# Both transformer layers as one pipeline of tiles, eight slots a turn, with a table-driven Gelu

## The reference

```
h = layernorm(x);   x = x + self_attention(h) @ w_ao + b_ao        # 16 heads of 16, sequences of 64
h = layernorm(x);   x = x + cross_attention(h, ctx) @ w_co + b_co  # keys and values from ctx
h = layernorm(x);   x = x + gelu_tanh(h @ w1 + b1) @ w2 + b2       # hidden width 1024
attention: softmax(q k^T / 4 * mask - 10000 (1 - mask)) v
gelu_tanh(u) = 0.5 u (1 + tanh(0.79788 u (1 + 0.044715 u^2)))
```

## Time and profile before

| | us |
|---|---|
| median of the runs | 1342.52 |
| the profiled execution | 1332.95 |
| its span, first to last instruction | 1331.1 |
| TensorE busy | 1135.1 (85%) |
| VectorE busy | 916.7 (69%) |
| ScalarE busy | 568.9 (43%) |
| GpSimd busy | 437.8 (33%) |
| mean granted TensorE clock | 0.954 of 2.4 GHz |

### The profile page before, as it was taken

The page is one execution under the profiler, slowest core; times in us unless marked ns, Lnnn a source line. Parts: engine busy times, 40 slices in busy tenths (PEclk is TensorE's granted clock), DMA queues, the critical chain, the costliest instruction groups (busy, mean ns, idle before and its releaser), DMA issues. The chain is left out here.

```text
span 1331.1 us, 21107 instructions
## 1 busy us (share of the span) xinstructions
PE 1135.1 (85%) x7616; PEld 679.9 (51%) x7616; DVE 916.7 (69%) x1677; ACT 568.9 (43%) x1053; POOL 437.8 (33%) x387
## 2 busy tenths in 40 slices
PE   6985678988988988988988988958698998989976
PEld 5653446655656655655755655744332442523414
DVE  4883658749749749759659759564358777595674
ACT  3552435635645645645545545524122324313322
POOL 2110425225225225225225234130135435253240
PEclk9997799999999999999999999989789898998987
DMA  6130010010010020030010010030100010010100
GB/s 225 56 91 12 1 37 1 6 49 1 17 37 29 17 81 1 17 112 1 17 37 1 17 37 2 1 133 1 47 1 18 1 32 18 0 34 0 32 0 17
DMA packets 36651, 41.27 MB, mean 31 GB/s; under 512 B 8000, under 2 KB 32320, under 8 KB 36304
## 3 DMA queue, kind: packets, MB, share of 16 engines
q1 hardware_dynamic: 36432, 39.81, 9.4%
q0 software_dynamic: 128, 0.10, 0.0%
HBM read 31.52 MB, written 8.39 MB: 30 GB/s over the span
## 5 line engine op out<-in xcount | busy, mean ns | idle before, releaser
L614 POOL TENSOR_TENSOR b_rstd<-b_var,b_minus_half 128x1 f32<-128x1 f32 x64 | 43.2, 674 | 275.6 <-DVE b_var L1078 275.6
L609 POOL TENSOR_TENSOR b_sc<-b_sc,b_cross_add 128x1024 f32<-128x1024 f32 x32 | 75.5, 2359 | 159.2 <-DVE b_sc L1112 159.2
L828 PE MATMUL ps<-w,b_act_g 128*128 128x256 f32 x512 | 117.7, 381 | 2.9 <-DVE b_act_g L1152 2.8
L816 PE MATMUL ps<-b_hT,wl 128*128 128x512 f32 x256 | 117.9, 606 | 1.6 <-ACT b_hT L931 1.6
L1440 POOL TENSOR_TENSOR c_rs<-c_st,c_rF 128x512 f32<-128x512 f32 x64 | 82.2, 1287 | 107.5 <-DVE c_st L1858 107.5
L828 PEld LDWEIGHTS ps<-w,b_act_g 128*128 128x128 f32 x512 | 95.4, 190 | 22.0 <-DVE b_act_g L1152 6.6
L948 ACT ACTIVATE b_sc<-b_sc 128x1024 f32<-128x1024 f32 x64 | 68.0, 1062 | 84.2 <-DVE b_sc L1121 84.2
L678 PE MATMUL ps<-b_hT,wl 128*128 128x512 f32 x192 | 90.0, 613 | 5.9 <-ACT b_hT L931 5.9
L1119 DVE TENSOR_REDUCE b_neg_max<-b_sc 128x16 f32<-128x1024 f32 x64 | 77.6, 1212 | 20.3 <-POOL b_sc L609 20.0
L1121 DVE TENSOR_TENSOR b_sc<-b_sc,b_neg_max 128x1024 f32<-128x1024 f32 x64 | 88.5, 1382 | 2.2
L765 PE MATMUL ps<-ident,b_sc 128*128 128x128 f32 x512 | 70.4, 283 | 21.8 <-ACT b_sc L948 21.8
(11 more groups left out here) (175 smaller groups left out, 2333.5 us busy)
## 6 DMA issues: line engine op xcount, KB each, us to landing
b_x_in<-x_mid SPq DMA_DIRECT2D x8, 512.0 KB, 3.9
enc<-in_ctxT SPq DMA_DIRECT2D x8, 512.0 KB, 4.0
x_mid<-b_x_out SPq DMA_DIRECT2D x8, 512.0 KB, 2.9
wl<-in_wl SPq DMA_DIRECT2D x2, 1280.0 KB, 9.4
area<-in_wc SPq DMA_DIRECT2D x1, 2272.0 KB, 8.2
a_x_in<-in_x SPq DMA_DIRECT2D x16, 128.0 KB, 2.4
a_y_in<-in_ctx SPq DMA_DIRECT2D x16, 128.0 KB, 2.5
wl<-in_wl SPq DMA_DIRECT2D x2, 1024.0 KB, 8.6
```

What stands on the lines that cost most here:

```text
L609: pool.tensor_tensor(t, t, m, ALU.add).then_inc(add_ok, 1)
L816: mm = pe.matmul(ps[:, YB + j % 2, :], weight("w1", k, j * P, (j + 1) * P), hT[:, k, :], start=(k == 0), stop=(k == NC - 1))
L828: mm = pe.matmul(ps[:, YB + p % 2, 0:D], act_g[:, j, p * P:(p + 1) * P], w["w2"][:, j, :], start=(j == 0), stop=(j == NJ - 1))
```

## The change

Only `phase_b` and the division of the weights into sets change.

- Order: a turn is eight slots, k = 0 to 7: self tiles 0 to 3, then cross tiles 4 to 7 of the same group. Each slot does `probs_T(k)`, `out_project(k-1)`, `times_v(k)`, `scores(k+2)`, `result_T(k)` on TensorE. The loop has six passes; the first and the last turn stand outside.
- The layernorm between self and cross attention is done by tile: `norm_T_mid` and `queries_mid` of tile k-1 stand in slots 1 to 4, in bank CO, with 128 columns.
- Work that fills the slots: context keys and values in slots 0 and 1, the first MLP matrix of the previous group (`hidden`) in slots 1 to 4, the next group's input projections in slots 4 to 6, `mlp_out` in slots 5 to 7.
- Gelu: VectorE adds the bias from PSUM into `act_g`; ScalarE does `Gelu_apprx_tanh` in place over four chunks (2048 columns) at a time, in slots 3 and 4. The factor 0.5 in `result` goes.
- On VectorE `subtract_max` becomes `maximum` and `subtract`, with `residual` of the tile before between them.
- New buffers: `x_res` (x plus bias, so `x_in` is free early), own input norm buffers, `xc` twice, three `hT` in place of one. `pre` and `poly` go.
- Four weight sets in place of three: `last` is divided into `out` and `hidden`. SyncE's loop is written out.

The diff, cut to its core:

```diff
-SETS = {"first": 3, "middle": 3, "last": 4}
+SETS = {"first": 3, "middle": 3, "out": 2, "hidden": 3}
...
 # sync, around the change of layers
+            load_mask(4, mask_rows[0])
+            load_enc(4, enc_cols[0])
+            load_x(5, rows[1])
+            for done, count in ((k_ok[1], 2 * NG), (v_ok[1], 2 * NG), (q_ok[1], 2 * NP * NG), (bias_ok[1], NP * NG)):
+                sp.wait_ge(done, count)
+            reload("middle")
+            store(2, rows[2])
+            mark_ready("middle", 1)
+            sp.wait_ge(o_ps, tile(NG, 0))
+            sp.wait_ge(bias_ok[2], NP * NG)
+            reload("out")
...
+            sp.wait_ge(m_ps, NP * NG)
+            sp.wait_ge(pre_ok, NJ * NG)
+            reload("hidden")
+            store(3, rows[3])
+            mark_ready("hidden", 1)
...
 # gpsimd
+            def turn(n, prev, nxt):
+                for k in range(TILES):
+                    if k >= 1:
+                        inv_std(n, k - 1)
+                    elif prev is not None:
+                        inv_std(prev, TILES - 1)
+                    if nxt is not None and k == 1:
+                        inv_std_in(nxt)
+                    if k + 2 < TILES:
+                        add_mask(n, k + 2)
+                    elif nxt is not None:
+                        add_mask(nxt, k + 2 - TILES)
+                    ... # add_bias(n, k - 2), add_bias_in(nxt, k - 2)
...
 # tensor
+            def queries_mid(n, p):
+                pe.wait_ge(h_ok[1], tile(n, 2 * p) + 2)
+                for c in range(NC):
+                    for k in range(NC):
+                        mm = pe.matmul(ps[:, CO, D + c * P:D + (c + 1) * P], weight("q2", k, c * P, (c + 1) * P),
+                                       hT_mid[:, k, p * P:(p + 1) * P], start=(k == 0), stop=(k == NC - 1))
+                mm.then_inc(q_ps[1], 1)
+            def mlp_out(n, p, nxt):
+                if p == 0:
+                    pe.wait_ge(g_ok, 2 * n + 2)
+                if nxt is not None:
+                    pe.wait_ge((k_ok, v_ok)[p // 2][0], 2 * nxt + p % 2 + 1)
...
+            # turn(n, prev, nxt); begin(k): probs_T(k), out_project(k-1); middle(k): times_v(k), scores(k+2);
+            # end(k): norm_T_mid(k-1) for k = 1..4, result_T(k)
+            # 0: begin keys_ctx(n,0) middle keys_ctx(n,1) end values_ctx(n,0)
+            # 1: begin values_ctx(n,1) middle norm_T_mlp(prev) end hidden(0) queries_mid(0)
+            # 2: begin hidden(1) middle hidden(2) end hidden(3) queries_mid(1)
+            # 3: begin hidden(4) middle hidden(5) end hidden(6) queries_mid(2)
+            # 4: begin hidden(7) middle norm_T_in(nxt) end queries_in(nxt,0) queries_mid(3)
+            # 5: begin queries_in(nxt,1) middle keys_in(nxt,0) end keys_in(nxt,1) mlp_out(prev,0)
+            # 6: begin mlp_out(prev,1) middle values_in(nxt,0) end values_in(nxt,1)
+            # 7: begin mlp_out(prev,2) middle mlp_out(prev,3) end
...
 # scalar
-            def pre_square(n, j): ...
-            def tanh(n, j): ...
+            def gelu(n, half):
+                j = slice(half * NJ // 2, (half + 1) * NJ // 2)
+                act.wait_ge(pre_ok, NJ * n + j.stop)
+                t = act_g[:, j, :].rearrange("f j t -> f (j t)")
+                act.activation(t, t, ACT.Gelu_apprx_tanh).then_inc(g_ok, 1)
+            # slot 0: copy_pT exps(1) keys(1,n,0) copy_cT keys(1,n,1)
+            # slot 1: copy_pT exps(2) norm_out(2,prev) norm_out_mid(0) copy_cT
+            # slot 2: queries_mid(0) copy_pT exps(3) norm_out_mid(1) copy_cT
+            # slot 3: queries_mid(1) copy_pT exps(4) gelu(prev,0) norm_out_mid(2) copy_cT
+            # slot 4: queries_mid(2) copy_pT exps(5) gelu(prev,1) norm_out(0,nxt) norm_out_mid(3) copy_cT
+            # slot 5: queries_in(nxt,0) queries_mid(3) copy_pT queries_in(nxt,1) exps(6) keys(0,nxt,0) copy_cT
+            # slot 6: copy_pT keys(0,nxt,1) exps(7) copy_cT;   slot 7: copy_pT exps(nxt 0) copy_cT
...
 # vector
-                dve.scalar_tensor_tensor(t, t, 1.0 / GELU_B, pre[:, j % 4, :], ALU.add, ALU.mult).then_inc(arg_ok, 1)
-                dve.scalar_tensor_tensor(act_g[:, j, :], poly[:, j % 4, :], 1.0, pre[:, j % 4, :], ALU.add, ALU.mult).then_inc(g_ok, 1)
+                dve.tensor_scalar(act_g[:, j, :], ps[:, YB + j % 2, :], vec("b1", j), None, ALU.add).then_inc(pre_ok, 1)
+            # every slot k: maximum(k+1) residual(k-1) subtract(k+1) norm(k-1) normalize(k) mask(k+2), and with it
+            # 0: cross_masks at the end; 1: values(1,n,0) behind maximum, values(1,n,1) behind norm, stats_in(nxt) at the end
+            # 2: pre(0) behind maximum, pre(1) behind norm, pre(2) norm_in(nxt) at the end; 3: pre(3), pre(4), pre(5) likewise
+            # 4: pre(6), pre(7); 6: result(prev,0), result(prev,1), values(0,nxt,0) at the end
+            # 7: values(0,nxt,1) behind maximum, result(prev,2) behind norm, result(prev,3) at the end
```

More of the change, by code:

```diff
@@ L662, in _, with add_bias_in @@
-            inv_std_first(0)
-            self_attention(0, None)
-            with pool.Fori(0, TURNS - 1) as it:
-                inv_std_first(it + 1)
-                cross(it, it + 1)
-                self_attention(it + 1, it)
-            cross(TURNS - 1, None)
+            def add_bias_in(n, p):
+                pool.wait_ge(ld_x, 16 * n + 16)
+                if p == 0:
+                    pool.wait_ge(ready["first"], n + 1)
+                after(pool, res_ok, tile(n - 1, p + 1))
+                pool.tensor_tensor(x_res[:, p, :], x_in[:, p, :], row("bao"), ALU.add).then_inc(bias_ok[0], 1)
@@ L670, in _ @@
+            inv_std_in(0)
+            for p in range(NP):
+                add_bias_in(0, p)
+            add_mask(0, 0)
+            add_mask(0, 1)
+            turn(0, None, 1)
+            with pool.Fori(1, TURNS - 1) as it:
+                turn(it, it - 1, it + 1)
+            turn(TURNS - 1, TURNS - 2, None)
+            add_bias(TURNS - 1, TILES - 2)
+            inv_std(TURNS - 1, TILES - 1)
+            add_bias(TURNS - 1, TILES - 1)
         @block.tensor
@@ L906, in _, with begin, middle @@
-            first_norm_T(0)
+                mm.then_inc(m_ps, 1)
+            def begin(n, k, prev):
+                probs_T(n, k)
+                if k >= 1:
+                    out_project(n, k - 1)
+                elif prev is not None:
+                    out_project(prev, TILES - 1)
+            def middle(n, k, nxt):
+                times_v(n, k)
+                if k + 2 < TILES:
+                    scores(n, k + 2)
+                elif nxt is not None:
+                    scores(nxt, k + 2 - TILES)
@@ L907, in _ @@
+            norm_T_in(0, None)
             for c in range(2):
-                queries_1(0, c)
+                queries_in(0, c)
             for c in range(2):
-                keys_1(0, c)
+                keys_in(0, c)
+            scores(0, 0)
             for half in range(2):
-                values_1(0, half)
-            for c in range(2):
-                keys_2(0, c)
-            self_attention(0, None)
-            with pe.Fori(0, TURNS - 1) as it:
-                cross(it, it + 1)
-                self_attention(it + 1, it)
@@ L919, in _ @@
-            cross(TURNS - 1, None)
+                values_in(0, half, None)
+            scores(0, 1)
+            turn(0, None, 1)
+            with pe.Fori(1, TURNS - 1) as it:
+                turn(it, it - 1, it + 1)
+            n = TURNS - 1
+            turn(n, n - 1, None)
+            out_project(n, TILES - 1)
+            norm_T_mlp(n, None)
+            for j in range(NJ):
+                hidden(n, j)
+            for p in range(NP):
+                mlp_out(n, p, None)
         @block.scalar
@@ L1055, in _ @@
+            norm_out(0, 0)
+            for c in range(2):
+                queries_in(0, c)
+            for c in range(2):
+                keys(0, 0, c)
+            exps(0, 0)
+            turn(0, None, 1)
+            with act.Fori(1, TURNS - 1) as it:
+                turn(it, it - 1, it + 1)
+            n = TURNS - 1
+            turn(n, n - 1, None)
+            norm_out(2, n)
+            gelu(n, 0)
+            gelu(n, 1)
         @block.vector
@@ L1154, in result, with norm @@
+            def norm(n, k):
+                p = k % NP
+                dve.wait_ge(rstd_ok, tile(n, k) + 1)
+                dve.tensor_scalar(xc[:, k // NP, p, :], x_cur[:, p, :], mv[:, p, 0:1], rstd[:, p:p + 1], ALU.subtract, ALU.mult).then_inc(xc_ok, 1)
             def result(n, p):
@@ new lines, in last_residual, with last_norm, next_mask @@
+            def last_residual(n, k, prev):
+                if k >= 1:
+                    residual(n, k - 1)
+                elif prev is not None:
+                    residual(prev, TILES - 1)
+            def last_norm(n, k, prev):
+                if k >= 1:
+                    norm(n, k - 1)
+                elif prev is not None:
+                    norm(prev, TILES - 1)
```

(25 more changed lines are left out.)

971 lines of the change are left out of this document (464 added, 507 removed).

## The result

The changed kernel took 1358.39 us (median of four, 1357.82 to 1360.45), the kernel before 1342.62 beside it: +15.8 us, a ratio of 1.0115 with a 95% interval of 1.0095 to 1.0135. It is slower, by little but clear of the noise. The forecast was 1350, +7.5.

The account below looks back on a forecast made before the run. TensorE's work plus the holes between it was taken to bound the turn. Six turns +16, opening -3, last turn and tail -7, weights +2 gave +8: 1341 us profiled, 1350 as median, range 1304 to 1374.

Parts of the forecast that it names:

- TensorE's work and holes in a turn: Steady turn of the changed kernel: 85.9 us of TensorE work plus 13.1 of holes, 99.0 in all.
- clock in a turn: Steady turn: 3.2 us at half speed behind the hole before queries_in(0), +1.6 us.
- opening: First turn: context keys move into slot 0, then VectorE's cycle sets the slots; -3 us, bounds -12 and +8.
- last turn and tail: From the last turn to the transformer phase's end: 121 us against 128.2, -7, bounds -12 and +5.
- from the profiled execution to the median: Median of the kernel before lay 9.6 us above its profiled execution; the same was added for the changed kernel.
- slot 4's hole: TensorE waits for hT_in behind ScalarE's exps(5), load, gelu(1), norm_out(0): 3.4 us, 2.1 to 3.4 with the load's bounds.
- another +1.6: Slot 6, behind the 2.7 us hole before mlp_out(1): upper bound for a clock loss, for which nothing was taken.
- The loop edge's 1.9: Hole on TensorE at each loop edge, expected to stay 1.9 us as in the kernel before.
- the 0.8: Middle queries as 32 matmuls of 128 columns instead of 8 of 512: +0.8 us of TensorE work a turn.
- the two rivals on it: Table switch drains: slot 4's hole 4.7, 1358 us, 7%. Gelu shares Exp's table or loads hidden: 2.1, 1333 us, 20%.
- the drain's rival: A table load on busy ScalarE costs 1.3 us more: slot 4's hole 4.7, +8, 1358 us, 7%.
- ScalarE doesn't hold TensorE: hT_in and keys come in time, so slots 4 to 6 close: turn 91.9 us, 1298 in all, 20%.

Follow-up runs that it names:

- The experiment with transposes: Changed kernel with twelve transposes of the identity, results never read, in each of two holes, ahead of queries_in(0) and the second mlp_out: 1346.3 us.
- Tanh: Changed kernel with Tanh in place of Gelu in the two activations of 2048 columns, which computes another function: 1339.5 us.
- subtract first: Changed kernel with subtract ahead of residual in each slot on VectorE: 1338.9 us.
- the two orders: Changed kernel with keys(0,nxt,1) ahead of copy_pT(6) and the second Gelu behind copy_pT(5), both on ScalarE: 1321.6 us.
- the 1290 us kernel: Changed kernel with the four orders, subtract ahead of residual on VectorE, and values(1,n,1) ahead of norm(0) in slot 1: 1290.1 us.
- four orders: Changed kernel: keys(0,nxt,1) before copy_pT(6), second Gelu after copy_pT(5), add_mask(n,3) before inv_std_in(nxt), weights "middle" released before store(2): 1309.2 us.

## Why the prediction was wrong in size

The way the changed kernel loses time is the one forecast: holes at the places named, by the order on ScalarE, and the clock behind them. What was wrong in size is the clock term. Point by point, against the traced executions:

| step | forecast | traced |
|---|---|---|
| TensorE's work and holes in a turn | 99.0 | 99.0 (87.8 + 11.2) |
| clock in a turn | 1.6 | 3.4 |
| a turn | 100.6 (+2.7) | 102.4 (+4.8) |
| six turns, with the wait for weights | +18 | +28.8 |
| opening | -3 | +0.6 |
| last turn and tail | -7 | -4.5 |
| sum | +8 | +24.9 |
| from the profiled execution to the median: before, changed | 9.6, 9.6 | 9.6, 0.6 |

*The clock* is the step that failed: +1.6 a turn was given, for one loss, and 3.4 is what it cost, for two. The prediction let slot 4's hole lose it because it was as long as one that had, and gave slot 6 nothing, because a hole of 2.52 had kept it. Slot 4's hole proved to be 2.53, not 3.4, and both lost it, slot 6's in five of six turns. The bound of "another +1.6" was there and was not taken; it is 11 of the 17 us by which the traced sum was missed (opening and tail are the other 6). The experiment with transposes shows the size, 3.2. The price of one loss, 1.6, was right: 1.5 in slot 4, 1.7 in slot 6. That one hole kept the clock was no ground for zero, and the trace of before said so: the prediction has its steady turns at a clock of 1.00 throughout, which holds for the turn of the earlier trace rows, while another lost it behind 1.92 us (row at 478.67 above).

*The holes.* The sum of 99.0 was right in part by luck, by terms that offset each other: work 85.9 and holes 13.1 forecast, 87.8 and 11.2 traced. The same fault is in the account of before, whose 85.1 of work and 12.8 of holes are 87.1 and 10.6 in the mean of its six traced turns, so the difference between the kernels came out right. (The hidden chunks in it are 8 x 1.75 = 14.0, not 14.3, and the six loop edges of before are 1.4 to 1.9, not 1.9 each.) Slots 0, 1, 5 and 6 came near what was laid out (0.45, 1.11 + 1.16, 1.03, 2.55). Slot 4 was 0.9 shorter: exps(5) ended 5.7 us into the slot and hT_in was there at 10.3, as forecast, but TensorE wanted it at 7.8 and not at 7.0, 0.47 of that being its own wait for VectorE before `norm_T_in`. Slot 3, for which none above 0.2 had been given, had 0.84 and 0.71. The first is add_mask late by inv_std_in: it went with that order. The second went with Tanh and with subtract first; the first Gelu stands ahead of norm_out_mid(2) there, which the list of ScalarE's order already showed. The loop edge's 1.9 did not come. The middle queries in 128 columns took 0.9 a tile and so cost nothing more, but all of TensorE's busy time at full clock is 87.8 where the earlier trace rows have 86.85; the 0.8 was about right, by luck, and where the 0.9 lies is open.

*The opening* was 3.6 worse: one hole of 5.67 in slot 2, in which 3.3 had been allowed; GpSimd's order accounts for 2.9. *The tail* gave 4.5 of the 7, and moves by more than that with the clock (above). *The weights* cost a hole of 1.79 once, as forecast, but the turn in which it lies is no longer than the others (102.48), since the clock was lost for less in it.

*The table loads.* One of 1.28 on the path, no drain: right, and the two rivals on it fall. That the drain's rival had 1358, where 1358.4 was measured, is chance: its hole of 4.7 is 2.53. *ScalarE doesn't hold TensorE* falls: the hole in slot 4 stands behind ScalarE's order. But the time it hoped for was there to be had: where the two orders were put right the turn fell to 95.1, and with the others to 91.6. That this is near the rival's 91.9 is chance too, since holes of 1.16 and 1.11 are left in slots 4 and 5 and the loop edge's has gone. ScalarE itself is busy 2.9 us less a turn and not 10, the four loads being 5.1 of its time.

*From the trace to the median.* The profiled execution of before was 9.6 under its median, and the prediction gave the changed kernel the same. The traced pair of before, 10.3 apart, shows what such a difference is made of: clock lost at edges and in the last half turn in one execution and not in the other. The changed kernel loses it at its two long holes in nearly every turn of both its traces, which fits its small spread. So this second error offset the first by luck: it took 9 us off the miss, and 24.9 traced became 15.8 measured.

Open: what decides whether one hole loses the clock; what sets the length of the third phase; that the wait at the loop edge is absent in the changed kernel; and in which place the 1290 us kernel's executions differ, of which one has a trace.

## What to carry to other kernels

Before a new order is forecast, count its holes on TensorE of the size of those that lost the clock in any turn (1.4 us and more here; holes of up to 1.16 never did in the steady turns of the kernels with four orders and more) and price each with a loss of its own (1.2 to 1.7 us), as likely as not, whatever a single hole of the same length did. Look at every turn of the trace for that, not at one. A hole that comes from one instruction out of place on an in-order engine is cheap to remove: four moved calls turned +15.8 us into -34. And take the changed stage's own time from the traces: the total carries 8 us and more from phases that no edit touches.
